# Powers of two and finished rows move from VectorE to GpSimd, and a help tile to a group without values

## The chip, the core and the metric

The kernel runs on one core of one Trainium2 chip. The metric is the time of one execution in device microseconds (us). Three executions of the kernel before took 615.28, 615.70 and 617.29 us, a median of 615.70. The profiled execution of the same kernel took 615.08 us, of which 613.3 us lie between its first and its last instruction (the span).

## The reference, cut to what matters

`x` has 4 batches of 1024 rows of 128 columns. Attention has 16 heads of 8 columns with a rotary embedding; the feed-forward part sends each row to the best 2 of 8 experts. Both start from the same normalised rows and are added to `x`:

```
xn = layernorm(x)
q, k, v = heads(xn @ Wq.T), heads(xn @ Wk.T), heads(xn @ Wv.T)   # 16 heads of 8 columns
q, k = rotary(q), rotary(k)
attn = softmax(einsum('bhnd,bhmd->bhnm', q, k) * 8 ** -0.5)
out = einsum('bhnm,bhmd->bhnd', attn, v)
gate = softmax(xn @ gate_w + gate_b);  top 2 of 8 experts per row
expert(x) = gelu(gelu(x @ w1 + b1) @ w2 + b2) @ w3 + b3
return x + out + sum(gate_k * expert_k(xn) for the two experts k)
```

## The kernel before, in words

Each engine runs one list of instructions, written out by hand and in that order; semaphores tie the lists together. Attention is done in 16 steps (`STEPS`): a step is one batch with four heads (`HG`), so four steps make a batch. Steps 0 to 8 come first, then the experts, then steps 9 to 15 (`SPLIT` is 9). The change is in the second part.

**A step from 9 on.** A step has 64 score tiles of 128 keys by 512 queries (two halves of the queries, 8 key tiles, 4 heads). TensorE (PE) makes scores for 60 of them in 20 groups of three (`late_scores`, L1748), each group into three PSUM banks of two sets that alternate. ScalarE (ACT) turns a group into exponentials with one instruction of 128x1536 (`late_exps`, L840). When a key tile's four heads are there, PE multiplies them with the values (`late_values`, L1780). The order on PE is: scores of group g+1, then values of the block that ended in group g-1. In groups 1, 5, 9, 13 and 17 no block of values is due; group 9 has the transposes of the previous step's output (`turn`, L1612) and group 17 the values of the help tiles.

**The help tiles.** The other 4 score tiles of a step (key tile 0 of the first half, four heads) go around ScalarE. PE scores them one at a time into the bank `aux_ps` (`help_scores`, L1763), in groups 0, 1, 3 and 4 (`HELP_GROUPS`). VectorE (DVE) reads each out with a scale and a shift (`read_help`, L1372), and a second one can be scored only when the first has been read. When all four are there, DVE computes 2 to the power of 128x2048 numbers with eight instructions (`help_exps`):

- k=0 (L1382): add a magic constant, so that the rounded exponent stands in the low bits
- k=1 (L1384): what remains after rounding
- k=2 (L1386): shift the bits by 23, which gives the power of two
- k=3 to 6 (L1388, four times): a polynomial of the remainder
- k=7 (L1390): the last term, times the power of two; it signals `help_made`

In group 17 PE waits for `help_made` and multiplies the help tiles with their values (`help_values`, L1790). Step 15 has three such tiles on DVE and one on ScalarE, in other groups (`LAST_HELP_GROUPS`), and does k=0 to 3 before and the rest after it copies half of the output (`copy_o`, L1067).

**DVE around it.** After the eight instructions DVE normalises the previous step (L1075, L1079), adds the experts' outputs of 6 row tiles to `x_all` (`combine`, L1331, twelve instructions), in steps 11, 12 and 13 adds the attention of batch 0, 1 and 2 to its rows (`finish_rows`, L1341), which the sync engine (SP) then stores, copies values (L965) and the output (L1067), and reads the next step's first help tile.

**GpSimd (POOL)** fetches in steps 9 to 14 the rows that `combine` needs: twelve indirect DMAs per step (four in step 14), in pairs that each wait for a block of values (`block_done`; L702).

Of the kernel before, what the change touches and what calls it, by code (L numbers as in the profile page):

```python
# [18 lines left out]
I32 = mybir.dt.int32  # L19
U32 = mybir.dt.uint32  # L20
ACT = mybir.ActivationFunctionType
ALU = mybir.AluOpType
# [5 lines left out]
HG = 4  # L28
# [109 lines left out]
HELP_GROUPS = (0, 1, 3, 4)  # L138
# [18 lines left out]
EXP_MAGIC = 1.5 * 2 ** 23 + 127 + 256  # L157
# [80 lines left out]
def build(nc, x, Wq, Wk, Wv, w1, b1, w2, b2, w3, b3, gw, gb, rope_cos, rope_sin, consts, out):  # L238
    ctx = ExitStack()
    with ctx:  # L240
# [131 lines left out]
        def group_probs(phase, g):  # L372
# [13 lines left out]
            o_copied norm_chain flag_made help_scored help_read help_chain help_made help_exp  # L386
# [7 lines left out]
                                                       "xs_in", "rope_loaded", "exchanged", "gathered"))  # L394

# [4 lines left out]
        def _(sp):  # L400
# [153 lines left out]
            for n, (tile, tiles) in enumerate([(b * BT, BT) for b in range(B - 1)] + [((B - 1) * BT, BT // 2)]):  # L554
                sp.wait_ge(S["out_ready"], n + 1)
                sp.dma_start(ov[:, tile // BT, tile % BT:tile % BT + tiles, :], xn_all[:, tile:tile + tiles, :]).then_inc(S["out_stored"], 16)
            sp.wait_ge(S["out_ready"], B + 1)
            sp.dma_start(ov[:, B - 1, BT // 2:BT, 0:DONE], xn_all[:, TILES - BT // 2:TILES, 0:DONE]).then_inc(S["out_stored"], 16)
            sp.wait_ge(S["out_ready"], B + 2)
# [18 lines left out]
        def _(pool):  # L578
# [283 lines left out]
        def _(dve):  # L862
# [472 lines left out]
            def finish_rows(tile, tiles):  # L1335

                b, k = tile // BT, tile % BT

                def rows(a):
                    return a[:, tile:tile + tiles, :].rearrange("p k (g c) -> p g k c", g=G)  # L1340
                return nc.vector.tensor_tensor(rows(xn_all), rows(x_all), attn_all[:, b * G:(b + 1) * G, k:k + tiles, :], ALU.add)  # L1341

# [32 lines left out]
            def help_exps(t, tiles, lo=0, hi=8):  # L1375

                n, done = tiles * HALF, (HG - tiles) * HALF
                scaled, rest, power = he_s[:, 0:n], he_g[:, 0:n], he_p[:, done:done + n]
                for k in range(lo, hi):
                    if k == 0:  # L1380
                        dve.wait_ge(S["help_read"], (t - SPLIT) * HG + tiles)
                        ins = nc.vector.tensor_scalar(power, scaled, EXP_MAGIC, None, ALU.add)  # L1382
                    elif k == 1:
                        ins = nc.vector.scalar_tensor_tensor(rest, power, EXP_MAGIC, scaled, ALU.subtract, ALU.subtract)  # L1384
                    elif k == 2:
                        ins = nc.vector.tensor_scalar(scaled.bitcast(I32), power.bitcast(I32), 23, None, ALU.logical_shift_left)  # L1386
                    elif k < 7:
# [5 lines left out]
                    dve.wait_ge(S["help_chain"], (t - SPLIT) * 7 + k + 1)  # L1393

            finished = {11: 0, 12: 1, 13: 2}
# [21 lines left out]
            help_exps(last, HG - 1, 0, 4)  # L1417
            normalise(last - 1)
            copy_o(last, 0)
            help_exps(last, HG - 1, 4)  # L1420
# [3 lines left out]
            finish_rows((B - 1) * BT, BT // 2).then_inc(S["out_ready"], 1)  # L1424
# [5 lines left out]
            with dve.If(dve.value_load(flag_i[0:1, 0:1], min_val=0, max_val=1)):  # L1430
# [20 lines left out]
                for b in range(B):  # L1451
                    finish_rows(b * BT, BT).then_inc(S["fb_ready"], 1)
# [492 lines left out]
```

## Time and profile before

| what | value |
|---|---|
| three executions | 615.28, 615.70, 617.29 us |
| profiled execution | 615.08 us, span 613.3 us |
| granted TensorE clock | 1.00 of full speed over the span |
| busy share of the span | PE 95%, ACT 90%, DVE 64%, POOL 44% |
| steps 9 to 15 | from 415 us to the end |

A row of the timeline view gives the start of an instruction, its duration, engine, line, operation, what it writes and reads with shapes, how many such instructions were merged into the row, and in square brackets the idle time of the engine before it and what ended that. Matmuls show two records each and overlap, so a busy PE says little by itself; the spacing of the rows says more.

### The profile page before, as it was taken

Reading aid. Unit: us, or ns where it says so; the run is one execution under the profiler, and the core shown is the slowest. Engines: PE = TensorE matmul, PEld = TensorE weight load, DVE = VectorE, ACT = ScalarE, POOL = GpSimd, SP = SyncE. Lnnn points to the kernel's source line nnn. Section 1 sums busy time; section 2 is a strip of 40 time slices with the busy share of each in tenths; the row PEclk is TensorE's granted clock in tenths of the full one; section 3 lists DMA queues with packets and bytes.
Section 4 is the critical chain, followed back from the end, with each engine's and each line's share of the span. In section 5 each row is a group of like instructions: output and inputs, shape, how many; then the busy total and the mean of one; then the engine's idle time right before and its main releaser. Section 6 shows DMA issues by size and latency. Waiting matters only on the chain.

```text
span 613.3 us, 12534 instructions
## 1 busy us (share of the span) xinstructions
PE 581.5 (95%) x4230; PEld 250.3 (41%) x4230; DVE 392.7 (64%) x796; ACT 553.6 (90%) x572; POOL 267.1 (44%) x258
## 2 busy tenths in 40 slices
PE   7889999999999998999899999998999999999996
PEld 5323332222222222222799999993222222222221
DVE  5754223865462424112688989856788989898866
ACT  3699999999999999999777777769999999999995
POOL 2700000000544545443366776653867758586100
PEclk9999999999999999999999999999999999999999
DMA  8564711641455446392544333311212122221311
GB/s 236 151 228 153 258 36 52 224 156 70 143 190 205 155 151 218 96 334 70 116 89 84 78 79 78 75 48 34 84 44 91 56 65 60 65 78 63 116 47 37
DMA packets 83297, 70.70 MB, mean 115 GB/s; under 512 B 45344, under 2 KB 59072, under 8 KB 83248
## 3 DMA queue, kind: packets, MB, share of 16 engines
q1 hardware_dynamic: 76528, 56.47, 30.8%
q0 software_dynamic: 5856, 13.05, 6.8%
q10 hardware_dynamic: 864, 0.58, 0.4%
q8 instruction: 24, 0.39, 0.3%
q14 instruction: 25, 0.20, 0.1%
HBM read 32.92 MB, written 32.96 MB: 107 GB/s over the span
## 4 chain that ended last, share of the span: by engine, by line
PE 59%; DVE 18%; ACT 12%; issue 8%; POOL 1%; DMA 1%; ACTq 0%; POOLq 0%; DVEq 0%; SPq 0%
PE ps L1716 14%; PE ps L1700 8%; DVE probs L1388 7%; PE ps L1648 7%; ACT probs L788 6%; PE ps L1631 5%; PE ps L1780 5%; PE ps L1663 5%; ACT probs L840 4%; PE ps L1599 4%; PE ps L1748 3%; ACT probs L766 2%; DVE probs L1390 2%; DVE x_all L1331 2%; PE ps L1544 2%
## 5 line engine op out<-in xcount | busy, mean ns | idle before, releaser
L788 ACT ACTIVATE probs<-ps 128x1536 f32<-128x1536 f32 (+1 forms) x154 | 204.9, 1439 | 3.1 <-PE ps L1700 3.0
L840 ACT ACTIVATE probs<-ps 128x1536 f32<-128x1536 f32 x140 | 189.8, 1514 | 1.5 <-PE ps L1748 1.3
L635 POOL DMA_INDIRECT slots_x_d<-xn_all,slot_i x64 | 64.3, 1004 | 190.5 <-PE ps L1716 180.1
L702 POOL DMA_INDIRECT work<-slots_y_d,slot_i x64 | 106.1, 1658 | 46.9 <-PE ps L1780 29.9
L1716 PE MATMUL ps<-probs,v_st 128*32 128x512 f32 x896 | 119.3, 605 | 0.6 <-ACT probs L788 0.6
L1780 PE MATMUL ps<-probs,v_st 128*32 128x512 f32 x840 | 111.4, 604 | 0.0
L805 ACT ACTIVATE work<-ps,work 128x256 f32<-128x256 f32 (+1 forms) x156 | 67.4, 455 | 30.6 <-PE ps L1648 23.4
L1700 PE MATMUL ps<-q_st,k_st 32*128 32x512 f32 x448 | 76.3, 494 | 5.9 <-ACT probs L788 5.7
L1748 PE MATMUL ps<-q_st,k_st 32*128 32x512 f32 x420 | 71.1, 494 | 7.3 <-ACT probs L840 6.9
L1700 PEld LDWEIGHTS ps<-q_st,k_st 32*128 32x128 f32 x448 | 28.9, 181 | 117.5 <-ACT probs L788 102.4
L1748 PEld LDWEIGHTS ps<-q_st,k_st 32*128 32x128 f32 x420 | 26.5, 181 | 106.1 <-ACT probs L840 98.3
L766 ACT ACTIVATE probs<-ps 128x1024 f32<-128x1024 f32 x64 | 60.6, 1035 | 4.9 <-PE ps L1579 4.2
L1648 PE MATMUL ps<-split 128*128 128x256 f32 x372 | 51.8, 289 | 0.0
L665 POOL TENSOR_TENSOR split<-parts,split 128x512 fp32r<-128x512 f32 x31 | 39.6, 1276 | 20.0 <-DVE split L1229 20.0
L1388 DVE SCALAR_TENSOR_TENSOR probs<-probs,work 128x2048 f32<-128x2048 f32 (+1 forms) x21 | 46.5, 2215 | 0.7
L1648 PEld LDWEIGHTS ps<-split 128*128 128x128 f32 x372 | 46.3, 190 | 0.0
L1631 PE MATMUL ps<-work 128*128 128x256 f32 (+1 forms) x156 | 38.3, 368 | 0.7 <-POOL work L659 0.3
L1663 PE MATMUL ps<-work 128*128 128x128 f32 x284 | 38.3, 276 | 0.1
L1663 PEld LDWEIGHTS ps<-work 128*128 128x128 f32 x284 | 37.3, 191 | 2.2 <-issue 0.5
L1599 PE MATMUL ps<-probs,v_st 128*32 128x512 f32 x256 | 34.1, 604 | 3.7 <-ACT probs L766 2.1
L679 POOL DMA_DIRECT2D slots_y_d<-work x39 | 27.3, 700 | 21.8 <-DVE work L1251 18.8
L1221 DVE TENSOR_TENSOR work<-b,zeros 128x4 f32<-128x4 f32 x39 | 32.0, 820 | 1.7 <-issue 1.7
(211 smaller groups left out, 640.8 us busy)
## 6 DMA issues: line engine op xcount, KB each, us to landing
k_d<-parts SPq DMA_DIRECT2D x8, 1024.0 KB, 5.3
q_d<-parts SPq DMA_DIRECT2D x8, 1024.0 KB, 6.2
q_st<-q_d SPq DMA_DIRECT2D x30, 256.0 KB, 3.5
k_st<-k_d SPq DMA_DIRECT2D x30, 256.0 KB, 2.6
slots_x_d<-parts SPq DMA_DIRECT2D x5, 1024.0 KB, 8.0
work<-slots_x_d SPq DMA_DIRECT2D x128, 32.0 KB, 1.9
slots_y_d<-work POOLq DMA_DIRECT2D x32, 128.0 KB, 2.3
work<-work SPq DMA_DIRECT2D x24, 128.0 KB, 2.0
```

Source lines behind the costliest of these rows:

```text
L702: nc.gpsimd.indirect_dma_start(out=gath[:, i % 2, GATHER * c + k, :], out_offset=None, in_=slots_y_d, in_offset=bass.IndirectOffsetOnAxis( ...
L766: nc.scalar.activation(probs[:, j % PROB_RING, 2 * pair:2 * pair + 2, :], score_slot(j, pair).rearrange("p (h n) -> p h n", h=2), ACT.Exp, ...
L788: nc.scalar.activation(group_probs(phase, g)[:, 0:size, :], group_slot(g)[:, 0:size * HALF].rearrange("p (h n) -> p h n", n=HALF), ACT.Exp ...
L840: nc.scalar.activation(late_probs(g), group_slot(g).rearrange("p (h n) -> p h n", n=HALF), ACT.Exp, scale=SCALE).then_inc(S["exp_done"], 1)
L1388: ins = nc.vector.scalar_tensor_tensor(power, rest if k == 3 else power, EXP_COEFFS[k - 3], rest, ALU.add, ALU.mult)
L1631: nc.tensor.matmul(h1_ps[m][:, 0:units * ST], w1_sb[:, n % 2, m * P:(m + 1) * P], xsT[:, n % 2, 0:units * ST], start=True, stop=True).then ...
L1648: ins = nc.tensor.matmul(h2_ps[m][:, 0:2 * ST], w[:, par, lo:lo + P], h[:, par, k * HID:k * HID + 2 * ST], start=(k == 0 and term == 0), s ...
L1663: ins = nc.tensor.matmul(y_ps[par][:, m, 0:C], h2[:, par, k, m * P:(m + 1) * P], w3_sb[:, par, k, :], start=(k == 0), stop=(k == 1))
L1700: ins = nc.tensor.matmul(group_slot(g)[:, n * HALF:(n + 1) * HALF], k_st[32 * h:32 * h + ROWS, mt * P:(mt + 1) * P], q_st[32 * h:32 * h + ...
L1716: ins = nc.tensor.matmul(o_ps[32 * h:32 * h + 32, :], v_window(mt, h, half), group_probs(phase, half * HALF_GROUPS + g)[:, n, :], start=(j ...
L1748: ins = nc.tensor.matmul(group_slot(g)[:, n * HALF:(n + 1) * HALF], k_st[32 * h:32 * h + ROWS, mt * P:(mt + 1) * P], q_st[32 * h:32 * h + ...
L1780: ins = nc.tensor.matmul(dst[32 * h:32 * h + 32, :], v_window(mt, h, half), late_probs(g)[:, k, :], start=begins, stop=ends)
```

## The change

Three things, all in steps 9 to 15. The powers of two (k=2) are made by GpSimd (`shift_help`), as a subtraction and a multiplication by 2^23 written as an integer, in place in the tile `he_p` that holds k=0's result; DVE's polynomial now runs in `he_s`, and only DVE's last instruction waits for GpSimd (`help_shifted`). GpSimd's instruction stands after its fourth indirect DMA of the step and waits until DVE has done k=1. The rows of batches 0, 1 and 2 are added by GpSimd, at the start of its lists for steps 12, 13 and 14, and SP stores them on a semaphore of their own (`rows_ready`). The fourth help tile of steps 9 to 14 is scored in group 5, which has no values, instead of group 4.

```diff
-HELP_GROUPS = (0, 1, 3, 4)
+HELP_GROUPS = (0, 1, 3, 5)
-EXP_MAGIC = 1.5 * 2 ** 23 + 127 + 256
+EXP_MAGIC = 1.5 * 2 ** 23 + 127
...
+            def shift_help(t, tiles):
+
+                power = he_p[:, (HG - tiles) * HALF:HG * HALF]
+                pool.wait_ge(S["help_chain"], (t - SPLIT) * 6 + 2)
+                nc.gpsimd.tensor_scalar(power.bitcast(I32), power, EXP_MAGIC - 127 + 256, float(2 ** 23), ALU.subtract, ALU.mult).then_inc(S["help_shifted"], 1)
+
             for i in range(STEPS - SPLIT - 1):
                 if i >= 2:
                     pool.wait_ge(S["combined"], i - 1)
+                if i >= 3:
+                    finish_rows(nc.gpsimd, (i - 3) * BT, BT).then_inc(S["rows_ready"], 1)
                 for k in range(min(GATHER, TILES - GATHER * i)):
                     block_done((SPLIT + i) * BLOCKS + 3 + 2 * k)
...
+                    if k == 1:
+                        shift_help(SPLIT + i, HG)
+            shift_help(STEPS - 1, HG - 1)
...
-                    elif k == 2:
-                        ins = nc.vector.tensor_scalar(scaled.bitcast(I32), power.bitcast(I32), 23, None, ALU.logical_shift_left)
-                    elif k < 7:
-                        ins = nc.vector.scalar_tensor_tensor(power, rest if k == 3 else power, EXP_COEFFS[k - 3], rest, ALU.add, ALU.mult)
+                    elif k < 6:
+                        ins = nc.vector.scalar_tensor_tensor(scaled, rest if k == 2 else scaled, EXP_COEFFS[k - 2], rest, ALU.add, ALU.mult)
                     else:
-                        nc.vector.scalar_tensor_tensor(power, power, EXP_COEFFS[4], scaled, ALU.add, ALU.mult).then_inc(S["help_made"], 1)
+                        dve.wait_ge(S["help_shifted"], t - (SPLIT - 1))
+                        nc.vector.scalar_tensor_tensor(power, scaled, EXP_COEFFS[4], power, ALU.add, ALU.mult).then_inc(S["help_made"], 1)
...
-                if t in finished:
-                    dve.wait_ge(S["combined"], t - SPLIT)
-                    finish_rows(finished[t] * BT, BT).then_inc(S["out_ready"], 1)
...
-            help_exps(last, HG - 1, 0, 4)
+            help_exps(last, HG - 1, 0, 3)
```

On DVE, a step's power of two before (`work` holds `he_s` and the remainder, `probs` the tile `he_p`):

```order
L1382 TENSOR_SCALAR probs<-work 128x2048
L1384 SCALAR_TENSOR_TENSOR work<-probs,work 128x2048
L1386 TENSOR_SCALAR work<-probs 128x2048
L1388 SCALAR_TENSOR_TENSOR probs<-work 128x2048
L1388 SCALAR_TENSOR_TENSOR probs<-probs,work 128x2048 x3
L1390 SCALAR_TENSOR_TENSOR probs<-probs,work 128x2048
```

and the same place after, with the instructions that follow:

```order
L1396 TENSOR_SCALAR probs<-work 128x2048
L1398 SCALAR_TENSOR_TENSOR work<-probs,work 128x2048
L1400 SCALAR_TENSOR_TENSOR work<-work 128x2048 x4
L1403 SCALAR_TENSOR_TENSOR probs<-work,probs 128x2048
L1097 RECIPROCAL o_rec<-ps 128x16 x2
L1101 TENSOR_TENSOR attn_all<-ps,o_rec 128x128 x2
```

One instruction of DVE is gone, and six instructions with two tensors in SBUF now stand in a row, where the third of eight had one.

On POOL, where before the list ends with one row of 64 indirect DMAs, the end of the list, from the middle of step 12 on, is now:

```order
L721 DMA work<-slots_y_d,slot_i 128x128 x8
L402 TENSOR_TENSOR xn_all<-x_all,attn_all 128x4x8x32
L721 DMA work<-slots_y_d,slot_i 128x128 x4
L711 TENSOR_SCALAR probs<-probs 128x2048
L721 DMA work<-slots_y_d,slot_i 128x128 x8
L402 TENSOR_TENSOR xn_all<-x_all,attn_all 128x4x8x32
L721 DMA work<-slots_y_d,slot_i 128x128 x4
L711 TENSOR_SCALAR probs<-probs 128x2048
L711 TENSOR_SCALAR probs<-probs 128x1536
```

The power of two stands behind four DMAs of its step, and eight DMAs and a batch's rows stand behind it.

On PE, groups 3 to 6 of step 9 before (L1763 is a help tile's score):

```order
L1748 MATMUL ps<-q_st,k_st 128x512 x3
L1763 MATMUL ps<-q_st,k_st 128x512
L1780 MATMUL ps<-probs,v_st 32x512 x4
L1748 MATMUL ps<-q_st,k_st 128x512 x3
L1763 MATMUL ps<-q_st,k_st 128x512
L1780 MATMUL ps<-probs,v_st 32x512 x4
L1748 MATMUL ps<-q_st,k_st 128x512 x6
L1780 MATMUL ps<-probs,v_st 32x512 x4
```

and after:

```order
L1757 MATMUL ps<-q_st,k_st 128x512 x3
L1772 MATMUL ps<-q_st,k_st 128x512
L1789 MATMUL ps<-probs,v_st 32x512 x4
L1757 MATMUL ps<-q_st,k_st 128x512 x3
L1789 MATMUL ps<-probs,v_st 32x512 x4
L1757 MATMUL ps<-q_st,k_st 128x512 x3
L1772 MATMUL ps<-q_st,k_st 128x512
L1757 MATMUL ps<-q_st,k_st 128x512 x3
L1789 MATMUL ps<-probs,v_st 32x512 x4
```

The fourth help tile stands one block of values and one group of scores later.

## Rows read from the trace of the kernel before

**Rows 1.** Page, section 1: busy us (share of span) and instructions per engine.

```profile
PE 581.5 (95%) x4230; PEld 250.3 (41%) x4230; DVE 392.7 (64%) x796; ACT 553.6 (90%) x572; POOL 267.1 (44%) x258
```

**Rows 2.** Timeline of ACT, one step's 20 exponentials.

```profile
505.05 27.12 ACT L840 ACTIVATE probs<-ps 128x1536 f32<-128x1536 f32 x20 [0.21 <-PE ps L1748]
```

**Rows 3.** Timeline of PE, end of step 10 and start of step 11.

```profile
466.51 1.06 PE L1790 MATMUL ps<-probs,v_st 128*32 128x512 f32 x8
467.51 0.50 PE L1748 MATMUL ps<-q_st,k_st 32*128 32x512 f32 x3
...
468.94 0.50 PE L1748 MATMUL ps<-q_st,k_st 32*128 32x512 f32 x3
...
475.44 0.50 PE L1748 MATMUL ps<-q_st,k_st 32*128 32x512 f32 x3
475.78 0.39 PE L1763 MATMUL ps<-q_st,k_st 32*128 32x512 f32 x1
```

**Rows 4.** Timeline of DVE, end of step 10 and step 11.

```profile
464.16 2.29 DVE L1390 SCALAR_TENSOR_TENSOR probs<-probs,work 128x2048 f32<-128x2048 f32 x1
...
476.93 1.23 DVE L1382 TENSOR_SCALAR probs<-work 128x2048 f32<-128x2048 f32 x1
...
480.52 1.23 DVE L1386 TENSOR_SCALAR work<-probs 128x2048 int32<-128x2048 int32 x1
481.78 2.29 DVE L1388 SCALAR_TENSOR_TENSOR probs<-work 128x2048 f32<-128x2048 f32 x1
...
491.09 2.29 DVE L1390 SCALAR_TENSOR_TENSOR probs<-probs,work 128x2048 f32<-128x2048 f32 x1
```

**Rows 5.** Timeline of DVE, the last help instruction of steps 9 and 14.

```profile
437.25 2.29 DVE L1390 SCALAR_TENSOR_TENSOR probs<-probs,work 128x2048 f32<-128x2048 f32 x1
...
573.05 2.29 DVE L1390 SCALAR_TENSOR_TENSOR probs<-probs,work 128x2048 f32<-128x2048 f32 x1
```

**Rows 6.** Timeline of DVE, a batch's rows in step 11.

```profile
497.63 1.23 DVE L1341 TENSOR_TENSOR xn_all<-x_all,attn_all 128x1024 f32<-128x1024 f32 x1
```

**Rows 7.** Timeline of PE, the second help tile of step 12.

```profile
499.65 0.50 PE L1763 MATMUL ps<-q_st,k_st 32*128 32x512 f32 x1 [0.42 <-DVE work L1372]
```

**Rows 8.** Timeline of POOL, indirect DMAs of steps 11 and 12.

```profile
482.17 2.72 POOL L702 DMA_INDIRECT work<-slots_y_d,slot_i  x1 [0.30 <-issue]
...
499.98 0.95 POOL L702 DMA_INDIRECT work<-slots_y_d,slot_i  x1 [0.30 <-issue]
505.27 1.03 POOL L702 DMA_INDIRECT work<-slots_y_d,slot_i  x1 [4.34 <-PE ps L1780]
```

**Rows 9.** Timeline of POOL among the experts.

```profile
299.53 1.26 POOL L665 TENSOR_TENSOR split<-parts,split 128x512 fp32r<-128x512 f32 x1 [4.91 <-DVE split L1229]
...
303.88 0.39 POOL L659 COPY work<-parts 128x256 f32 x1
```

**Rows 10.** Timeline of DVE among the experts.

```profile
299.61 1.20 DVE L1221 TENSOR_TENSOR work<-b,zeros 128x4 f32<-128x4 f32 x1
...
301.07 0.67 DVE L1242 TENSOR_TENSOR split<-work,split 128x512 fp32r<-128x512 f32 x1
...
304.07 0.74 DVE L1242 TENSOR_TENSOR split<-work,split 128x512 fp32r<-128x512 f32 x1
```

**Rows 11.** DVE's line L1221: duration ns min/median/max.

```profile
L1221 DVE TENSOR_TENSOR work<-b,zeros x39: 114/1201/1227, 279.5 to 406.4; 128x4 f32<-128x4 f32 x39
```

**Rows 12.** POOL's groups by line and shape: busy us, mean ns of one.

```profile
L659 POOL COPY work<-parts 128x256 f32 x39 | 15.6, 400 | 8.2 <-PE ps L1631 5.6 <-issue 2.6
...
L581 POOL MEMSET parts<- 128x2048 f32 x1 | 1.8, 1812 | 0.0
...
L624 POOL CAST parts<-work 128x512 fp32r<-128x512 f32 x1 | 0.6, 611 | 0.1
```

**Rows 13.** Timeline of DVE, the copy of half the output in step 15.

```profile
595.68 0.69 DVE L1067 COPY o_sb<-ps 128x512 f32<-128x512 f32 x1 [2.32 <-PE ps L1780]
```

**Rows 14.** Timeline of PE, the help tiles' values in step 15.

```profile
603.57 1.07 PE L1790 MATMUL ps<-probs,v_st 128*32 128x512 f32 x8 [0.78 <-DVE probs L1390]
```

More of the change, by code:

```diff
@@ L385, in build @@
             st_init ka_loaded kb_loaded q0_loaded q1_loaded v_loaded scores_done exp_done pv_done
-            o_copied norm_chain flag_made help_scored help_read help_chain help_made help_exp
+            o_copied norm_chain flag_made help_scored help_read help_chain help_shifted help_made help_exp rows_ready
             w_loaded b12_made w1_made w2_made w2_low_made w3_made h1_high_made h1_low_made xs_in0 xs_in1 xs_in2 xs_in3 xsT_made
@@ L394, in build, with finish_rows, rows @@
                                                        "xs_in", "rope_loaded", "exchanged", "gathered"))
+        def finish_rows(engine, tile, tiles):
+            b, k = tile // BT, tile % BT
+            def rows(a):
+                return a[:, tile:tile + tiles, :].rearrange("p k (g c) -> p g k c", g=G)
+            return engine.tensor_tensor(rows(xn_all), rows(x_all), attn_all[:, b * G:(b + 1) * G, k:k + tiles, :], ALU.add)
         block = ctx.enter_context(nc.Block())
@@ L554, in _ @@
             for n, (tile, tiles) in enumerate([(b * BT, BT) for b in range(B - 1)] + [((B - 1) * BT, BT // 2)]):
-                sp.wait_ge(S["out_ready"], n + 1)
+                if n < B - 1:
+                    sp.wait_ge(S["rows_ready"], n + 1)
+                else:
+                    sp.wait_ge(S["out_ready"], 1)
                 sp.dma_start(ov[:, tile // BT, tile % BT:tile % BT + tiles, :], xn_all[:, tile:tile + tiles, :]).then_inc(S["out_stored"], 16)
-            sp.wait_ge(S["out_ready"], B + 1)
+            sp.wait_ge(S["out_ready"], 2)
             sp.dma_start(ov[:, B - 1, BT // 2:BT, 0:DONE], xn_all[:, TILES - BT // 2:TILES, 0:DONE]).then_inc(S["out_stored"], 16)
-            sp.wait_ge(S["out_ready"], B + 2)
+            sp.wait_ge(S["out_ready"], 3)
             sp.dma_start(ov[:, B - 1, BT // 2:BT, DONE:C], xn_all[:, TILES - 4:TILES, DONE:C]).then_inc(S["out_stored"], 16)
@@ L1333, in combine @@
                     ins.then_inc(S["combined" if c else "comb_chain"], 1)
[L1335 to L1341, printed above, removed]
             def finish_early_columns():
@@ L1373, in read_help, with help_exps @@
                         .then_inc(S["help_read"], 1)
-            def help_exps(t, tiles, lo=0, hi=8):
+            def help_exps(t, tiles, lo=0, hi=7):
                 n, done = tiles * HALF, (HG - tiles) * HALF
@@ L1384, in help_exps @@
                         ins = nc.vector.scalar_tensor_tensor(rest, power, EXP_MAGIC, scaled, ALU.subtract, ALU.subtract)
-                    elif k == 2:
-                        ins = nc.vector.tensor_scalar(scaled.bitcast(I32), power.bitcast(I32), 23, None, ALU.logical_shift_left)
-                    elif k < 7:
-                        ins = nc.vector.scalar_tensor_tensor(power, rest if k == 3 else power, EXP_COEFFS[k - 3], rest, ALU.add, ALU.mult)
-                    else:
-                        nc.vector.scalar_tensor_tensor(power, power, EXP_COEFFS[4], scaled, ALU.add, ALU.mult).then_inc(S["help_made"], 1)
+                    elif k < 6:
+                        ins = nc.vector.scalar_tensor_tensor(scaled, rest if k == 2 else scaled, EXP_COEFFS[k - 2], rest, ALU.add, ALU.mult)
+                    else:
+                        dve.wait_ge(S["help_shifted"], t - (SPLIT - 1))
+                        nc.vector.scalar_tensor_tensor(power, scaled, EXP_COEFFS[4], power, ALU.add, ALU.mult).then_inc(S["help_made"], 1)
                         return
                     ins.then_inc(S["help_chain"], 1)
-                    dve.wait_ge(S["help_chain"], (t - SPLIT) * 7 + k + 1)
-            finished = {11: 0, 12: 1, 13: 2}
+                    dve.wait_ge(S["help_chain"], (t - SPLIT) * 6 + k + 1)
             read_help(SPLIT, 0, 1)
@@ L1416, in _ @@
             read_help(last, 0, HG - 1)
-            help_exps(last, HG - 1, 0, 4)
+            help_exps(last, HG - 1, 0, 3)
             normalise(last - 1)
             copy_o(last, 0)
-            help_exps(last, HG - 1, 4)
+            help_exps(last, HG - 1, 3)
             combine(last - SPLIT - 1)
@@ L1423, in _ @@
             dve.wait_ge(S["combined"], last - SPLIT)
-            finish_rows((B - 1) * BT, BT // 2).then_inc(S["out_ready"], 1)
+            finish_rows(nc.vector, (B - 1) * BT, BT // 2).then_inc(S["out_ready"], 1)
             finish_early_columns().then_inc(S["out_ready"], 1)
@@ L1451, in _ @@
                 for b in range(B):
-                    finish_rows(b * BT, BT).then_inc(S["fb_ready"], 1)
+                    finish_rows(nc.vector, b * BT, BT).then_inc(S["fb_ready"], 1)
         @block.tensor
```

## The prediction, made before the changed kernel ran

> **What bounds the kernel now.** I read the page's busy times first: PE 95%, ACT 90%, DVE 64%, POOL 44% [rows 1]. They don't say what bounds steps 9 to 15, so I read those by the timelines. ACT does the 20 exponentials of a step in 27.12 us with 0.21 us of waiting [rows 2]; the reader is to see an engine that is nearly full. But a loop of PE and DVE closes in the same time, and the change works on that loop. I follow it from step 10 into step 11. Call M the moment at which DVE's last help instruction ends. M of step 10 is 464.16 + 2.29 = 466.45 [rows 4]; PE starts the help tiles' values at 466.51 [rows 3], so it takes them just in time. From there PE's groups with values follow each other 1.43 us apart (467.51 to 468.94), the scores made in group 4 start at 475.44, the fourth help tile at 475.78 [rows 3]. DVE starts k=0 at 476.93, 1.15 us after that tile, and ends k=7 at 491.09 + 2.29 = 493.38 [rows 4], which is M of step 11: 26.93 us after the last. From M of step 9 (437.25 + 2.29 = 439.54) to M of step 14 (573.05 + 2.29 = 575.34) there are 135.80 us [rows 5], five such periods with a mean of 27.16. That mean is higher because in steps 11, 12 and 13 DVE adds a batch's rows, 1.23 us [rows 6], after which PE waits 0.42 us for a help tile to be read [rows 7]: 5 x 26.93 = 134.65, and the other 1.15 us are those three. So all three engines need about the same time. A longer DVE chain is paid in full, a shorter one gives little.
>
> **The fourth help tile in group 5.** It is scored after the scores that stand one group later. Those start at 475.44 + 1.43 = 476.87; with the same 0.34 us from scores to help tile (475.78 - 475.44) and the same 1.15 us to k=0, k=0 starts at 478.36, which is 1.43 us later than before.
>
> **k=2 leaves DVE.** From its start to the next instruction's are 481.78 - 480.52 = 1.26 us [rows 4]. The two edits together bring M of step 11 to 493.38 + 1.43 - 1.26 = 493.55, if nothing else happens: a period of 27.10 us.
>
> **The power of two on GpSimd.** The question is whether it runs beside DVE. Behind k=1, DVE now has five instructions in a row that each read two tensors in SBUF, with 0.03 us between them, and GpSimd's is issued behind its fourth DMA, in the middle of them. What happens when the two engines meet is in the trace, in both directions. GpSimd's indirect DMA takes 0.95 us when DVE does something else and 2.72 us beside a polynomial instruction [rows 8]: it ends at 484.89, 0.82 us after DVE's instruction that ended at 481.78 + 2.29 = 484.07 [rows 4]. So it was held from 0.13 us after its start to the end of DVE's instruction, and then got in although the next one stood 0.03 us behind. In the other direction, DVE's addition of two 128x4 tensors, 114 ns at best [rows 11], starts at 299.61 inside a GpSimd addition that ends at 300.79 and lasts 1.20 us [rows 9, 10], to 300.81. A GpSimd copy with one input holds DVE too: it ends at 304.27, and DVE's subtraction that starts at 304.07 takes 0.74 us in place of 0.67 [rows 9, 10], ending 0.54 us after the copy. So I expect GpSimd to wait for the end of a polynomial instruction, then to hold the next one off until it is done. It costs the same wherever among the five it lands, since each waits for the one before it.
>
> The price: with S the duration of GpSimd's instruction alone, it holds DVE for S - 0.13. DVE's next instruction has by then done 0.67 - 0.54 = 0.13 us of its start, and lay 0.03 us behind anyway. DVE loses B = S - 0.29. No row shows S. The nearest are one-input instructions of GpSimd: a copy of 128x256 in 0.40 us, a cast of 128x512 in 0.61 and a memset of 128x2048 in 1.81 [rows 12]. From the first two, 256 columns cost 0.21 us, so 2048 cost 0.61 + 6 x 0.21 = 1.87. I take that, as it is near the memset of the same size: B = 1.58. From above, at the rate of GpSimd's addition, 4 x 1.26 = 5.04 us [rows 9], B = 4.75. From below B = 0, if the two run beside each other. A gain is excluded for this term, because DVE's last instruction waits for the result.
>
> The Trainium skill (SBUF — State Buffer, Who interferes with whom) has a rule for this: a VectorE instruction with two SBUF inputs and any GpSimd instruction that reads SBUF exclude each other, and who issues first keeps the other out for the whole instruction. The copy's row agrees, but with 0.07 us only. By the rule the sum is the one below; if GpSimd's one-input instructions were exempt, it would be the first rival's.
>
> **The batches' rows on GpSimd.** Three additions of 128x1024, each 2 x 1.26 = 2.5 us [rows 9]. GpSimd ends a step's DMAs at 500.93 and starts the next at 505.27, after 4.34 us without work [rows 8]. The power of two pushes one DMA (0.95 + 0.30) more behind M, which leaves about 3.1 us. In this stretch DVE reads help tiles from PSUM. So I cost it at nothing; without that cover it would hold k=0 off by up to 2.5 us in three steps. On DVE the 1.23 us go, and with them PE's waits: that is the 1.15 us above, which the new period of 27.10 us doesn't contain.
>
> **Step 15.** k=2 goes there too, but DVE waits 2.32 us for the copy of the output behind it [rows 13], so the time saved is waited. GpSimd's instruction (1536 columns, 0.61 + 4 x 0.21 = 1.45 us) falls into the same wait. The rest of the chain comes after the copy, and PE's wait of 0.78 us [rows 14] stays. I count 0; without that cover, 1.45 us. SP's stores of three batches are far from the end.
>
> **The sum.** M of step 9 comes 0.17 + B later. Five periods of 27.10 + B replace 135.80: -0.30 + 5B. Together -0.13 + 6B = 9.35 us with B = 1.58. The profiled execution took 615.08 us, so the changed one takes 624.4; the median of the runs is 0.62 us above it, which gives 625.0.
>
> **Rivals.**
> 1. Not slower: GpSimd's instruction, with one input, runs beside DVE, or in the pauses of its start-ups. B = 0 gives -0.13 us, 615.6. For it: the row of the copy shows little. Against it: the DMA rows, where a small read of GpSimd waited for the whole instruction of DVE. It decides from B = 0.33 on (6B - 0.13 is then 0.3%).
> 2. Slower still: making an integer out of a float takes GpSimd longer than a cast. Half way between the bounds, S = 3.46, B = 3.17, 18.9 us more: 634.6. For it: two arithmetic operations and a conversion that no row shows. Against it: cast and memset run at the same 0.8 to 0.9 ns per column. The Trainium skill (GPSIMD Engine Reference, Elementwise — side-by-side cycle accounting) gives about 1.8 cycles of 1.2 GHz per element as a loop's best case: an estimate of 3.07 us, with which the sum would be 632.3. By that, the cast of 512 columns would last 0.77 us, and the trace has 0.61, so I hold the rule not to apply to one input.
> 3. Faster: B = 0, and the fourth help tile runs beside the group's scores, without the 0.34 us, in six steps: -0.13 - 2.04 = -2.2 us, 613.5. For it: the other help tiles run beside theirs. Against it: the fourth one did not in group 4, and B must vanish too.
>
> **Numbers.** The forecast has a chance of 0.65, rival 1 of 0.12, rival 2 of 0.17, rival 3 of 0.06. What a measurement of this kernel can tell from no change is about 0.3%, 1.8 us. So faster 0.06, within 0.3% 0.12, slower 0.82. The forecast's own range is 623 to 629 (S from 1.81 to 2.5). The range of 615.5 to 635 takes in about half of rival 1 and most of rival 2, and leaves out rival 3: 18% in all. Predicted: 625.0 us.
>
> **What would show it.** In the changed kernel's profile one of the polynomial instructions of each step should last about 3.9 us in place of 2.29, and end 2.15 us after GpSimd's instruction; k=7 and the rest 2.29. PE should wait some 1.7 us for DVE before the help tiles' values, and ACT as long. M to M should be 28.7 us. The batches' rows on GpSimd should end before DVE's k=0, and PE's 0.42 us should be gone. The prediction is wrong in its main step if all five stay at 2.29 us while GpSimd works; wrong in size if GpSimd's instruction is held by DVE longer than one instruction or takes much over 2 us after it; and wrong in the loop if M comes later without ACT waiting.

## The result, and the profile after

The changed kernel takes 661.0 us (median of 6 runs, 660.5 to 665.1), the kernel before 615.6 us beside it. The ratio is 1.074, with an interval of 1.0726 to 1.0762. The forecast was 625.0 us and the range ended at 635: the direction was right, and the 45.4 us are almost five times the 9.4 us of the sum. The profiled execution took 660.5 us with a span of 658.7 us, before 613.3.

From the page of the changed kernel: the busy times that answer to [rows 1], the granted clock in 40 slices (in tenths, 9 for nine tenths or more), and the groups of GpSimd's new instruction and of PE's help values (busy, mean ns of one, then the idle time ahead of the group and what ended most of it):

```profile
PE 598.6 (91%) x4230; PEld 252.8 (38%) x4230; DVE 411.9 (63%) x786; ACT 555.3 (84%) x572; POOL 315.5 (48%) x268
...
PEclk9999999999999999999999999998979796979799
...
L711 POOL TENSOR_SCALAR probs<-probs 128x2048 int32<-128x2048 f32 (+1 forms) x7 | 57.5, 8218 | 20.3 <-DVE work L1398 20.1
...
L1799 PE MATMUL ps<-probs,v_st 128*32 128x512 f32 x56 | 12.7, 995 | 28.0 <-DVE probs L1403 28.0
```

There is much in these rows that the forecast did not have. GpSimd's instruction lasts 8.2 us in the mean of its two sizes where about 2 were assumed; some 1.5 of them are waiting, as the next rows show. PE waits 28.0 us for DVE ahead of the help tiles' values, in seven waits. PE has the same 4230 rows of matmuls as before and is busy 17.1 us longer with them, and behind step 9 its clock falls below nine tenths of full speed in every second slice. Two of the four executions of the kernel with the power of two alone, below, took 657.6 and 657.8 us at a granted clock of 0.951, where the other two had 0.972 and 0.975; they are left out.

The end of step 10 in DVE's timeline, which answers to [rows 4] (start, duration, x4 is four instructions in a row):

```profile
458.77 1.23 DVE L1396 TENSOR_SCALAR probs<-work 128x2048 f32<-128x2048 f32 x1
460.03 2.29 DVE L1398 SCALAR_TENSOR_TENSOR work<-probs,work 128x2048 f32<-128x2048 f32 x1
462.36 13.45 DVE L1400 SCALAR_TENSOR_TENSOR work<-work 128x2048 f32<-128x2048 f32 x4
475.84 2.29 DVE L1403 SCALAR_TENSOR_TENSOR probs<-work,probs 128x2048 f32<-128x2048 f32 x1
```

GpSimd in the same stretch, which answers to [rows 8]:

```profile
463.45 2.02 POOL L721 DMA_INDIRECT work<-slots_y_d,slot_i  x1 [0.30 <-issue]
465.50 8.44 POOL L711 TENSOR_SCALAR probs<-probs 128x2048 int32<-128x2048 f32 x1
```

Four polynomial instructions of 2.29 us, with three gaps of 0.03, would take 9.25 us. They take 13.45: DVE loses 4.2 us. The second of the four runs from 462.36 + 2.32 = 464.68 to 466.97. GpSimd starts inside it at 465.50, waits 1.47 us to its end, and then works 6.97 us, to 473.94. The third and the fourth by themselves show which one is held:

```profile
467.01 6.47 DVE L1400 SCALAR_TENSOR_TENSOR work<-work 128x2048 f32<-128x2048 f32 x1
473.52 2.29 DVE L1400 SCALAR_TENSOR_TENSOR work<-work 128x2048 f32<-128x2048 f32 x1
```

The fourth starts 0.42 us before GpSimd's instruction ends and still takes its 2.29.

PE at the end of that step, which answers to [rows 3]:

```profile
473.41 0.50 PE L1757 MATMUL ps<-q_st,k_st 32*128 32x512 f32 x3
478.19 1.93 PE L1799 MATMUL ps<-probs,v_st 128*32 128x512 f32 x8 [4.28 <-DVE probs L1403]
480.05 0.80 PE L1757 MATMUL ps<-q_st,k_st 32*128 32x512 f32 x3
480.78 1.94 PE L1789 MATMUL ps<-probs,v_st 128*32 128x512 f32 x8
...
484.74 0.50 PE L1757 MATMUL ps<-q_st,k_st 32*128 32x512 f32 x3
```

The four matmuls of values (two rows each, x8) take 1.93 us behind the wait, 1.06 before the change [rows 3]; three of scores take 0.80 and not 0.50. The busy times of four stretches tell why (stretch; its length, then PE, PEld, DVE, ACT, POOL; granted clock, DMA share, GB/s):

```profile
465.00:473.00 8.00, 7.42 (x62) 1.92 (x58) 7.97 (x2) 8.00 (x8) 7.97 (x2) 1.00 0.15 41
474.00:478.00 4.00, 0.00 (x0) 0.00 (x0) 3.97 (x2) 1.78 (x2) 3.59 (x2) 0.92 0.06 16
478.20:483.00 4.80, 4.80 (x22) 0.97 (x22) 4.18 (x17) 1.45 (x1) 3.60 (x4) 0.50 0.28 73
485.00:500.00 15.00, 14.45 (x112) 4.08 (x112) 10.68 (x10) 14.66 (x12) 7.78 (x7) 1.00 0.13 39
```

The granted clock is 1.00 (2.4 GHz) up to the wait and falls before the wait is over (0.92 in the mean of 4.0 us of it, in which PE does nothing). It is 0.50 (1.2 GHz) in the 4.8 us behind the wait although PE is busy in all of them, and 1.00 again later. The Trainium skill (TensorE: Matmul & The Clock Gate, Part 1: The HAM clock gate) says that the slow clock is the array's default and that activity lifts it. These rows agree: they show the two levels, the slow one behind a stretch without matmuls and the fast one again after work.

### The profile page after: what moved, and what is told of

The parts are those of the page before. It is cut to its first block, busy times and chain, and to the rows that moved or that the text cites. A ratio compares the mean times of both kernels' runs of the same rounds, so it can differ in the third digit from the quotient of the medians.

```text
span 658.7 us, 12538 instructions
## 1 busy us (share of the span) xinstructions
PE 598.6 (91%) x4230; PEld 252.8 (38%) x4230; DVE 411.9 (63%) x786; ACT 555.3 (84%) x572; POOL 315.5 (48%) x268
## 4 chain that ended last, share of the span: by engine, by line
PE 58%; DVE 23%; ACT 10%; issue 6%; POOL 1%; DMA 1%; POOLq 0%; ACTq 0%; DVEq 0%; SPq 0%
DVE work L1400 13%; PE ps L1725 12%; PE ps L1709 7%; PE ps L1789 7%; ACT probs L810 6%; PE ps L1657 6%; PE ps L1640 4%; PE ps L1672 4%; PE ps L1757 3%; PE ps L1608 3%; DVE probs L1403 2%; DVE work L1398 2%; PE ps L1799 2%; ACT probs L788 2%; PE ps L1553 1%
## 5 line engine op out<-in xcount | busy, mean ns | idle before, releaser
L1725 PE MATMUL ps<-probs,v_st 128*32 128x512 f32 x896 | 119.3, 605 | 0.6 <-ACT probs L810 0.6
L1789 PE MATMUL ps<-probs,v_st 128*32 128x512 f32 x840 | 119.1, 643 | 0.1
L721 POOL DMA_INDIRECT work<-slots_y_d,slot_i x64 | 90.5, 1414 | 48.7 <-PE ps L1789 33.5
L1400 DVE SCALAR_TENSOR_TENSOR work<-work 128x2048 f32<-128x2048 f32 (+1 forms) x28 | 87.1, 3111 | 0.9
L1709 PE MATMUL ps<-q_st,k_st 32*128 32x512 f32 x448 | 76.3, 494 | 5.9 <-ACT probs L810 5.7
L1757 PE MATMUL ps<-q_st,k_st 32*128 32x512 f32 x420 | 74.3, 520 | 7.3 <-ACT probs L862 6.9
L1709 PEld LDWEIGHTS ps<-q_st,k_st 32*128 32x128 f32 x448 | 28.9, 181 | 117.5 <-ACT probs L810 102.4
L711 POOL TENSOR_SCALAR probs<-probs 128x2048 int32<-128x2048 f32 (+1 forms) x7 | 57.5, 8218 | 20.3 <-DVE work L1398 20.1
L1386 DVE TENSOR_SCALAR work<-ps 128x512 f32<-128x512 f32 x27 | 18.6, 690 | 40.4 <-PE ps L1772 40.4
L1799 PE MATMUL ps<-probs,v_st 128*32 128x512 f32 x56 | 12.7, 995 | 28.0 <-DVE probs L1403 28.0
```

The lines of the kernel that those rows point to most:

```text
L721: nc.gpsimd.indirect_dma_start(out=gath[:, i % 2, GATHER * c + k, :], out_offset=None, in_=slots_y_d, in_offset=bass.IndirectOffsetOnAxis( ...
L1400: ins = nc.vector.scalar_tensor_tensor(scaled, rest if k == 2 else scaled, EXP_COEFFS[k - 2], rest, ALU.add, ALU.mult)
L1709: ins = nc.tensor.matmul(group_slot(g)[:, n * HALF:(n + 1) * HALF], k_st[32 * h:32 * h + ROWS, mt * P:(mt + 1) * P], q_st[32 * h:32 * h + ...
L1725: ins = nc.tensor.matmul(o_ps[32 * h:32 * h + 32, :], v_window(mt, h, half), group_probs(phase, half * HALF_GROUPS + g)[:, n, :], start=(j ...
L1757: ins = nc.tensor.matmul(group_slot(g)[:, n * HALF:(n + 1) * HALF], k_st[32 * h:32 * h + ROWS, mt * P:(mt + 1) * P], q_st[32 * h:32 * h + ...
L1789: ins = nc.tensor.matmul(dst[32 * h:32 * h + 32, :], v_window(mt, h, half), late_probs(g)[:, k, :], start=begins, stop=ends)
```

## The experiments

Six runs take parts of the change, or remove one suspected cost from it; one measures GpSimd's instruction in other forms; the last is a version that came out of them. Where a run was timed, the kernel before had 615.4 or 615.6 us (median) beside it.

**The power of two alone**, with k=2 made by GpSimd, and the rows and the fourth help tile left as before:

```
-EXP_MAGIC = 1.5 * 2 ** 23 + 127 + 256
+EXP_MAGIC = 1.5 * 2 ** 23 + 127
...
+                power = he_p[:, (HG - tiles) * HALF:HG * HALF]
+                pool.wait_ge(S["help_chain"], (t - SPLIT) * 6 + 2)
+                nc.gpsimd.tensor_scalar(power.bitcast(I32), power, EXP_MAGIC - 127 + 256, float(2 ** 23), ALU.subtract, ALU.mult).then_inc(S["help_shifted"], 1)
...
```

> The kernel before with the power of two on GpSimd alone (group 4 and the batches' rows as before). Theory A (GpSimd's instruction is the cost: the changed kernel's trace has it at 6.97 us after its hold, and the DVE instruction beside it 4.19 us longer): DVE's chain becomes 4.19 - 1.26 = 2.93 us longer, PE waits about 3 us before the help tiles' values, six times: 615.1 + 17.6 = 633 at full clock, and up to 2.7 us per step more, 649, if the clock falls after that wait as it does after 4.3 us in the changed kernel. Rival B (the group is the cost, GpSimd's instruction is only waited for because everything is late): within 3 us of before.

Measured: 647.9 and 648.4 us, too few for an interval; their mean is 1.053 of before. This edit alone carries most of the loss, and the time is near the upper end of what was expected, with the fallen clock. PE waits 3.4 to 3.6 us per step, and DVE's held instruction lasts 6.5 us. PE's timeline at the end of step 10:

```profile
477.46 1.93 PE L1801 MATMUL ps<-probs,v_st 128*32 128x512 f32 x8 [3.38 <-DVE probs L1401]
```

DVE's last help instruction there:

```profile
475.11 2.29 DVE L1401 SCALAR_TENSOR_TENSOR probs<-work,probs 128x2048 f32<-128x2048 f32 x1 [0.55 <-POOL probs L711]
```

Without the later help tile GpSimd's instruction lands one polynomial instruction further back in DVE's chain. Its end comes later against that chain, and DVE's last instruction waits 0.55 us for it in each of six steps. So it does matter where among the five it lands.

**The fourth help tile in group 5, alone:**

```
-HELP_GROUPS = (0, 1, 3, 4)
+HELP_GROUPS = (0, 1, 3, 5)
```

> The kernel before with the fourth help tile in group 5 alone. Theory A: DVE's chain starts 1.43 us later in six steps, PE waits 1.4 us, five periods of 28.36 in place of a mean of 27.16, and 1.43 in step 9: 7.4 us more, 622.5, at full clock. Rival B (the group is the larger part of the loss): over 20 us more, 636 or above. Rival C (a group without values relieves PE, whose scores of group 6 come 0.2 us earlier): 1 us less, 614.

Measured: 633.0 us (627.2 to 634.5), 1.025 [1.019, 1.031]. That is 10.5 us above the expectation. The periods from M to M are 28.9 to 30.0 us, and 28.36 would be the old one with the 1.43 us of the later tile. PE's rows and the busy times at the end of step 10 show what was left out. First PE's timeline:

```profile
472.54 1.07 PE L1790 MATMUL ps<-probs,v_st 128*32 128x512 f32 x8 [1.37 <-DVE probs L1390]
...
473.97 1.93 PE L1780 MATMUL ps<-probs,v_st 128*32 128x512 f32 x8
```

Then the busy times of the same place:

```profile
472.50:478.00 5.50, 5.46 (x34) 1.07 (x34) 4.23 (x17) 3.23 (x3) 4.28 (x5) 0.69 0.47 143
```

A wait of 1.37 us is enough here: one group still runs at full clock (1.07 us), the next takes 1.93, and the mean clock of the 5.5 us is 0.69. It isn't so every time. At the end of step 11 a wait of 1.48 us leaves the clock at 1.00. PE's timeline and the busy times there:

```profile
502.57 1.07 PE L1790 MATMUL ps<-probs,v_st 128*32 128x512 f32 x8 [1.48 <-DVE probs L1390]
```

```profile
502.50:508.00 5.50, 5.43 (x45) 1.34 (x45) 5.36 (x19) 4.29 (x4) 4.28 (x5) 1.00 0.43 143
```

In this execution the clock falls within 2 us of the start of the help tiles' values in four of the six steps. The four executions go from 627.2 us with a mean clock of 0.994 to 634.5 with 0.983. What decides between the two isn't known.

**The batches' rows alone:**

```
+                if i >= 3:
+                    finish_rows(nc.gpsimd, (i - 3) * BT, BT).then_inc(S["rows_ready"], 1)
...
-            finished = {11: 0, 12: 1, 13: 2}
...
```

> The kernel before with the three batches' rows on GpSimd alone. Theory A: DVE loses 1.23 us in three steps and PE's wait of 0.42 us goes; GpSimd's additions start 7.5 us after the last help instruction, when DVE's value copies are done (6.3 us after it), so they hold nothing: 1.15 us less, 614. Rival D (GpSimd's addition holds DVE's value copy, as in the changed kernel, where L987 takes 2.0 us in place of 0.22): 1.1 us more in each of three steps, 617 to 618.

Measured: 614.35 us (9 runs), 0.998 [0.9967, 0.9993]. The five periods are 26.90 to 26.93 us; the 1.15 us that the prediction gave to these rows came back.

**The wait filled.** The changed kernel, with ten matmuls whose moving operand and weights are zeros, added to what stands in PSUM, ahead of PE's wait for the help tiles (the trace has two rows for each):

```
+FILLERS = 10
...
+                if not last:
+                    for _ in range(FILLERS):
+                        nc.tensor.matmul(o_ps[0:32, 0:HALF // 2], zeros[:, 0:32], zeros[:], start=False, stop=False)
                 pe.wait_ge(S["help_made"], t - (SPLIT - 1))
```

> The changed kernel with ten matmuls of zeros (128x256, added to the output's bank, where they change nothing) on PE ahead of its wait for the help tiles, in steps 9 to 14. They take about as long as the wait of 4.3 us. Theory A (the clock falls because PE stands still in the wait): the granted clock stays at 1.0, the 2.7 us per step that PE loses after the wait at half clock are gone, 16 us less, and the batches' rows no longer meet the value copies, up to 3 us less: 642 to 645. Rival E (the clock falls for another reason, or the time after the wait is lost to something else): 661.

Measured: 641.4 us (640.3 to 642.6), 1.041 [1.039, 1.043]. PE has more to do and the kernel is 19.6 us faster than the changed one. DVE's chain is as long as ever. PE's timeline at the same place:

```profile
473.20 4.50 PE L1799 MATMUL ps<-zeros 128*32 128x256 f32 x20
477.55 1.06 PE L1803 MATMUL ps<-probs,v_st 128*32 128x512 f32 x8
478.55 0.51 PE L1758 MATMUL ps<-q_st,k_st 32*128 32x512 f32 x3
```

And the busy times behind the wait:

```profile
477.50:483.00 5.50, 5.50 (x47) 1.36 (x46) 4.96 (x19) 3.84 (x3) 4.28 (x5) 1.00 0.46 141
```

The values take 1.06 us again, the clock is 1.00, and all five periods are 31.25 to 31.40 us. PE still starts the values 0.06 us behind M, as in the kernel before (466.51 for 466.45), so the zeros fill the wait and don't lengthen it.

**The group alone, filled** with three such matmuls (FILLERS = 3 in the kernel with HELP_GROUPS = (0, 1, 3, 5)):

> The kernel before with the fourth help tile in group 5, and three matmuls of zeros ahead of PE's wait in steps 9 to 14, about as long as the 1.4 us wait. Theory A (the group costs 1.43 us per step through DVE's chain, and what it lost above that, up to 633, was the clock after the wait): clock 1.0, periods of 28.36, 622.5. Rival (the group costs more by itself): 627 to 633 as without the zeros.

Measured: 624.5 us (624.3 to 626.1), 1.014 [1.012, 1.016]: 8.5 of the 17.5 us came from the clock, in the medians. 9.0 are left, and 7.4 were expected. The periods are 28.35 and 28.46 us in the first two, as worked out, and 28.85 in the three in which DVE still adds a batch's rows, where PE still waits 0.37 us for DVE. Those three times 0.49 us are the 1.5 that the expectation lacked.

**The rows back on DVE**, in the otherwise changed kernel:

```
-                if i >= 3:
-                    finish_rows(nc.gpsimd, (i - 3) * BT, BT).then_inc(S["rows_ready"], 1)
...
+                if t in finished:
+                    dve.wait_ge(S["combined"], t - SPLIT)
+                    finish_rows(nc.vector, finished[t] * BT, BT).then_inc(S["rows_ready"], 1)
...
```

> The changed kernel with the batches' rows back on DVE in steps 11 to 13. Theory A (at half clock PE frees the output so late that DVE's value copy falls into GpSimd's addition, which holds it 2 us): the periods of steps 12 to 14 fall from 35.16 to 34.0, 3.4 us less than the changed kernel in all, 657.5. Rival (those periods are longer for another reason): 661, or more by 1.23 us per step, 664.

Measured: 658.1 us (657.4 to 659.8), 1.068 [1.066, 1.071]. So in the changed kernel the move of the rows costs 2.9 us, where alone it gains 1.1. The total was as expected; the periods were not (33.3, 35.4, 33.3, 35.2, 33.2 in turn). The long ones are those in which the clock comes back late. The stretches from 4 to 8 us behind M of step 10 (a long period) and of step 11 (a short one):

```profile
481.51:485.51 4.00, 4.00 (x23) 0.95 (x23) 0.36 (x3) 1.67 (x2) 3.08 (x4) 0.50 0.55 170
516.88:520.88 4.00, 3.80 (x34) 0.93 (x30) 2.87 (x6) 3.19 (x4) 3.09 (x4) 0.97 0.57 170
```

Why it comes back late in every second step stays open. As the clock's share differs too, the 2.9 us are a difference of two totals and not the price of the collision alone. The collision itself is in the changed kernel's timelines. DVE at step 12:

```profile
521.01 2.00 DVE L987 COPY v_st<-v_all 128x128 f32<-128x128 f32 x1
522.93 0.68 DVE L1386 TENSOR_SCALAR work<-ps 128x512 f32<-128x512 f32 x1
```

GpSimd there:

```profile
520.54 2.37 POOL L402 TENSOR_TENSOR xn_all<-x_all,attn_all 128x1024 f32<-128x1024 f32 x1
```

In the kernel with the rows alone, the same copy of DVE in the same step comes ahead of the addition:

```profile
500.84 0.22 DVE L984 COPY v_st<-v_all 128x128 f32<-128x128 f32 x1
```

And GpSimd's addition there:

```profile
501.88 2.39 POOL L402 TENSOR_TENSOR xn_all<-x_all,attn_all 128x1024 f32<-128x1024 f32 x1
```

The copy of V, from SBUF to SBUF, takes 0.22 us alone and 2.00 when GpSimd's addition has started; it ends at 523.01, 0.10 us behind the addition, the help tile's read waits behind it, and PE waits 0.76 us for that read. In step 14 of the changed kernel it takes 2.91 us, though it starts 0.44 us ahead of the addition, beside an indirect DMA of GpSimd that ends at 590.86. DVE and then GpSimd there:

```profile
590.43 2.91 DVE L987 COPY v_st<-v_all 128x128 f32<-128x128 f32 x1
```

```profile
590.87 2.37 POOL L402 TENSOR_TENSOR xn_all<-x_all,attn_all 128x1024 f32<-128x1024 f32 x1
```

What held the copy before 590.87 stays open.

**Other instructions in the place of GpSimd's.** In the filled kernel each step has another one:

```
+                form = t - SPLIT
+                if form in (0, 6):
+                    ins = nc.gpsimd.tensor_scalar(power.bitcast(I32), power, EXP_MAGIC - 127 + 256, float(2 ** 23), ALU.subtract, ALU.mult)
+                elif form == 1:
+                    ins = nc.gpsimd.tensor_scalar(power, power, EXP_MAGIC - 127 + 256, float(2 ** -23), ALU.subtract, ALU.mult)
+                elif form == 2:
+                    ins = nc.gpsimd.tensor_scalar(power, power, EXP_MAGIC - 127 + 256, None, ALU.subtract)
+                elif form == 3:
+                    ins = nc.gpsimd.tensor_copy(power.bitcast(I32), power)
+                elif form == 4:
+                    ins = nc.gpsimd.tensor_copy(power, power)
+                else:
+                    ins = nc.gpsimd.tensor_tensor(power, power, he_g, ALU.mult)
...
```

> The filled kernel with another GpSimd instruction of 128x2048 in place of the power of two in each step, so that the help tiles' probabilities of steps 10 to 14 aren't the reference's: step 9 as it was (subtract, multiply, float to integer), 10 the same with a float result, 11 a subtraction alone, 12 a copy float to integer, 13 a copy float to float, 14 a multiplication of two tensors. Theory F1 (making integers is slow): step 10 about 1.9 us after its hold, step 12 as slow as step 9's 7.0. Theory F2 (two arithmetic operations with constants are slow, at 3.4 ns a column): steps 9 and 10 both 7.0, step 11 between 1.9 and 7.0, steps 12 and 13 about 1.9, step 14 about 4 to 5. In both, DVE's polynomial instruction is held by each of them, and by the copies for 1.6 us (B = S - 0.29 with S = 1.87), while the hold by step 9 is 4.2 and not 6.7, which neither explains.

Measured: 645.2 us, in a single execution, so each form stands for one instruction. GpSimd's groups by line and shape (busy, mean ns of one, idle before):

```profile
L714 POOL TENSOR_SCALAR probs<-probs 128x2048 int32<-128x2048 f32 x1 | 8.4, 8429 | 0.0
L716 POOL TENSOR_SCALAR probs<-probs 128x2048 f32<-128x2048 f32 x1 | 8.4, 8429 | 0.0
...
L718 POOL TENSOR_SCALAR probs<-probs 128x2048 f32<-128x2048 f32 x1 | 6.7, 6718 | 0.0
L724 POOL TENSOR_TENSOR probs<-probs,work 128x2048 f32<-128x2048 f32 x1 | 5.9, 5912 | 0.0
L720 POOL CAST probs<-probs 128x2048 int32<-128x2048 f32 x1 | 3.2, 3249 | 0.0
L722 POOL COPY probs<-probs 128x2048 f32<-128x2048 f32 x1 | 3.2, 3248 | 0.0
```

DVE's four polynomial instructions in steps 10, 11 and 12, beside two operations, one operation and a cast:

```profile
459.65 13.45 DVE L1414 SCALAR_TENSOR_TENSOR work<-work 128x2048 f32<-128x2048 f32 x4
...
491.04 12.60 DVE L1414 SCALAR_TENSOR_TENSOR work<-work 128x2048 f32<-128x2048 f32 x4
...
526.93 10.84 DVE L1414 SCALAR_TENSOR_TENSOR work<-work 128x2048 f32<-128x2048 f32 x4
```

Each GpSimd instruction begins inside a polynomial instruction and stands still for some 1.5 us; S is what is left. What DVE loses is the held instruction's duration less 2.29:

| GpSimd's instruction, 128x2048 | S, us | DVE loses, us | S − 0.29 |
|---|---|---|---|
| subtract and multiply, to int32 | 6.97 | 4.19 | 6.68 |
| subtract and multiply, to f32 | 6.95 | 4.18 | 6.66 |
| subtract | 5.24 | 3.33 | 4.95 |
| tensor by tensor | 4.42 | 4.25 | 4.13 |
| cast to int32, and copy | 1.75 | 1.57 | 1.46 |

A cast costs what a copy does, and the two-operation form costs the same to float as to int32: the conversion adds nothing. The tensor-scalar instruction does. With 1.75 us for a copy, its form with one operation takes three times as long and that with two four times. It isn't arithmetic as such, for the product of two tensors takes 4.42. Nor is it DVE beside it: in step 15 of the changed kernel GpSimd's instruction has 1536 columns and works from 635.34, the end of DVE's instruction that it waits for, to 640.58, and DVE is idle in all but 0.9 us of that.

```profile
633.63 6.95 POOL L711 TENSOR_SCALAR probs<-probs 128x1536 int32<-128x1536 f32 x1 [20.15 <-DVE work L1398]
```

Those 5.24 us are three quarters of 6.97.

For copy, cast and tensor by tensor, DVE loses S but for 0.18 us, which is the forecast S − 0.29 within 0.12. Beside the tensor-scalar forms it loses less. If DVE stands still first and then goes on at its own speed, it is held for 4.35 of GpSimd's 6.97 us (2.16 us of its 2.29 would lie behind the hold), and for 3.49 of 5.24. The rows don't show whether it stands still first or is slow throughout; they do show that the next instruction of DVE isn't held at all.

**The rows on GpSimd, and DVE's copy in step 15 one instruction later.** The batches' rows as above, and in step 15 one polynomial instruction more ahead of DVE's copy of the output, in DVE's wait:

```
-            help_exps(last, HG - 1, 0, 4)
+            help_exps(last, HG - 1, 0, 5)
             normalise(last - 1)
             copy_o(last, 0)
-            help_exps(last, HG - 1, 4)
+            help_exps(last, HG - 1, 5)
```

> The rows on GpSimd alone, and in step 15 one more polynomial instruction of DVE ahead of its copy of the output, where it waits 2.3 us. If PE's wait of 0.78 us in step 15 is DVE's chain behind that copy, it goes, and 0.5 to 0.8 us with it: 613.6, a ratio of 0.9965 to before. If the end is set by something else: 614.4 as with the rows alone.

Measured: 613.8 us (12 runs), 0.9974 [0.9959, 0.9988]: 1.8 us under the kernel before, the fastest version here. DVE in step 15, which answers to [rows 13]:

```profile
591.42 1.76 DVE L1399 SCALAR_TENSOR_TENSOR probs<-probs,work 128x1536 f32<-128x1536 f32 x1
...
595.90 0.69 DVE L1086 COPY o_sb<-ps 128x512 f32<-128x512 f32 x1 [1.80 <-PE ps L1787]
596.51 3.54 DVE L1399 SCALAR_TENSOR_TENSOR probs<-probs,work 128x1536 f32<-128x1536 f32 x2
```

PE's wait of 0.78 us [rows 14] is gone:

```profile
602.95 1.06 PE L1797 MATMUL ps<-probs,v_st 128*32 128x512 f32 x8
```

The gain over the rows alone, 0.6 us, lies inside the intervals of the two.

## Why the prediction was wrong

**Where the 45.4 us are.** M of step 9 comes 4.85 us later (444.39 for 439.54). The five periods to M of step 14 take 173.30 us, 135.80 before [rows 5]: 37.50. The rest of the span adds 3.0. By cause:

- DVE held: 6 x 4.19 − 0.13 = 25.0 us. The filled wait shows this alone: 641.4 is 25.9 over before, and its periods of 31.26 are the prediction's 27.10 and 4.16.
- PE's clock behind steps 9, 10 and 14. With 4.19 a period at full clock would be 31.29. The first two are 33.74 and 34.07, and from M of step 14 to that of step 15 it is 30.97 us for 28.08 before: 2.45 + 2.78 + 2.89 = 8.1 us.
- PE's clock and the batches' rows, behind steps 11, 12 and 13. These periods are 35.16, 35.17 and 35.16 us, 11.6 over 31.29 in all.

The last two are 19.7, and 0.7 us are left, 0.5 of them in M of step 9. Filling the wait gave 19.6 back. It has taken both together, since with the clock at 1.00 DVE's copy comes ahead of GpSimd's addition again (514.98 and 517.28 us in step 12). How the 11.6 us are shared can't be read off, for the three periods are alike while the clock in them is not:

| behind M of step | granted clock, 4 to 8 us behind M | GpSimd's addition ends | DVE's copy takes | and ends |
|---|---|---|---|---|
| 11 | 0.74 | 522.91, 10.71 behind M | 2.00 us | 523.01 |
| 12 | 0.50 | 558.07, 10.71 behind M | 0.93 us | 558.17 |
| 13 | 1.00 | 593.24, 10.71 behind M | 2.91 us | 593.34 |

In these steps GpSimd's addition sets the pace: it ends at the same distance behind M whatever the clock, and DVE's copy 0.10 us behind it. The late clock behind step 12 is hidden by it, and behind step 13 it costs its time although the clock is back.

**The first step that failed is the term S.** "I take that, as it is near the memset of the same size": 1.87 us was right for a copy (1.75) and a wrong neighbour for a subtraction and a multiplication, at 6.97. So B was 4.19 and not 1.58: six times 2.61 are 15.7 of the 36.0 us by which the forecast was too low. Even the bound above, S = 5.04 from the addition of two tensors, was too low, though a one-input instruction seemed sure to be below a two-input one. The prediction had named this sign of being wrong in size, a GpSimd instruction that takes much over 2 us. Rival 2 had the right sign, mostly for the wrong reason: it blamed the conversion to an integer, which costs nothing, and had the two operations for support only. The Trainium skill (GPSIMD Engine Reference, Engine selection) calls one-input instructions on GpSimd roughly line-rate. The copy's 1.75 us bear that out against DVE's 1.23 for a tensor-scalar instruction of the same size [rows 4], and GpSimd's own tensor-scalar instruction does not, at 5.7 times DVE's.

**The second is a term that was missing: PE's clock.** It is most of the 19.7 us: with the rows back on DVE, where the copy of V meets no addition of GpSimd, 2.9 of them go. The prediction saw that PE would wait, "some 1.7 us", and counted the wait alone. The run with the group alone shows that waits of 1.4 to 2.1 us bring the clock down in four of six steps, at 8.5 us over the same kernel with the wait filled. So the sum would likely have been too low even with S as it was taken: 625.0 and 8.5 make some 633.5, an estimate from that run.

**The rule B = S − 0.29** fell for this form: 4.19 and not 6.68. Two misses pulled against each other here, and so it was luck that B came out inside its bound of 4.75 although S did not. That DVE is held for the whole of GpSimd's instruction is also what the Trainium skill says (SBUF — State Buffer, Who interferes with whom). It is so for the copy, the cast and the two-tensor form, and not for the tensor-scalar forms, beside which DVE loses 4.19 of 6.97 us and 3.33 of 5.24. How GpSimd leaves DVE that time stays open.

**"In this stretch DVE reads help tiles from PSUM"** left out DVE's copies of V, which go from SBUF to SBUF and stand between those reads. With the rows moved alone they lie clear of GpSimd's addition; in the changed kernel they do not. Nor did PE's wait for the second help tile go there, 0.42 us before [rows 7]: it is 0.76 us in step 12 and 1.67 in step 14.

**"It costs the same wherever among the five it lands"** held in the changed kernel only. With the power of two alone GpSimd's instruction lands one instruction later, and DVE's last one waits 0.55 us for its end.

**A sum.** The range of 623 to 629 is not what S from 1.81 to 2.5 gives by the prediction's own formula, 624.7 to 628.8.

**What held.** The direction did, and the loop. GpSimd waits to the end of one polynomial instruction and gets in ahead of the next; the loop of PE and DVE pays for it in full, and ACT, which waited 0.21 us in a step [rows 2], waits with PE. Its timeline of the changed kernel, at the end of step 10:

```profile
480.90 1.45 ACT L862 ACTIVATE probs<-ps 128x1536 f32<-128x1536 f32 x1 [5.11 <-PE ps L1757]
```

The later help tile and the shorter chain cost +1.43 and −1.26: the filled wait's periods bear out the 27.10. Step 15 is free: GpSimd's instruction works 5.24 us there where 1.45 were assumed, and still ends (640.58) ahead of the copy of the output that DVE waits for (640.92).

## What to carry to other kernels

Before work moves to an engine, find a row of that engine with the same operation, and where there is none, let the range reach past the nearest one: the duration of a copy says little of a tensor-scalar instruction of the same shape (1.75 and 6.97 us here). In a stretch where TensorE is nearly full, a new wait of one or two microseconds can cost twice, once as itself and once as half the clock behind it; zeros multiplied into the accumulator are a quick way to tell the two apart, and to get the second back. Moved work is free on an engine with idle time only while no instruction of a neighbour that it holds off comes due then, and that is to be asked again when the step grows longer.

## What was not expected of the hardware

- GpSimd's tensor-scalar instruction on 128x2048 f32 takes 5.24 us with one operation and 6.97 with two, more than its product of two tensors (4.42).
- DVE's instruction with two inputs loses 4.19 us beside the 6.97 of such a GpSimd instruction, but all of a copy's or a product's time but 0.18 us.
- GpSimd's instruction gets in between two polynomial instructions of DVE that stand 0.03 us apart, in each of steps 9 to 14.
- The granted clock fell to 0.50 after a wait of 4.28 us in a stretch where PE was otherwise busy; after one of 1.37 us the next group was still fast and the one behind it slow, 1.93 for 1.07 us; after one of 1.48 us in the same run it stayed at 1.00. With the wait filled by zeros it stayed at 1.00 in every step.
